# The last of an answer's twelve copies of transposed probabilities: from ScalarE to VectorE

## The reference

```
x = x + attention_0(x)    # layer norm, 16 heads of 64, one shared key/value head, a bias of 16x256x256,
                          # a mask of keys, a null key and value, a causal mask, softmax, output projection, norm
x = x + attention_1(x)    # the same form; q and k are normalized, the bias comes from a small MLP over distances
x = x + experts_2(x)      # 8 experts of 64 and a shared one of 128, two experts to a token
x = x + experts_3(x)
```

## Time and profile before

| | us |
|---|---|
| median of 3 runs | 357.94 |
| lowest, highest run | 357.38, 360.69 |
| the profiled execution, its own time | 356.2 |
| its span, first to last instruction | 354.4 |
| PE busy | 326.2 (92%) |
| DVE busy | 253.0 (71%) |
| ACT busy | 246.3 (69%) |
| POOL busy | 195.5 (55%) |

### The profile page before, as it was taken

One profiled execution on the slowest core, in us unless ns is written; L12 is line 12 of the kernel. 1 busy time (PEld: TensorE's weight loads), 2 busy tenths in 40 slices (PEclk: granted clock), 3 DMA queues, 4 the chain that ended last, 5 costly groups with the idle time before them and its releaser, 6 DMA issues.

```text
span 354.4 us, 7089 instructions
## 1 busy us (share of the span) xinstructions
PE 326.2 (92%) x2276; PEld 245.7 (69%) x2276; DVE 253.0 (71%) x917; ACT 246.3 (69%) x822; POOL 195.5 (55%) x282
## 2 busy tenths in 40 slices
PE   8789989997989999989997899989999899999996
PEld 6676756677667767766676567666767578676885
DVE  4668998896756677948785888578769536477672
ACT  2679876996788778969895879697886922232330
POOL 4591186479358866977498769786943502200000
PEclk9999999999999999999999999999999999999999
DMA  5961202320839500219110202021120200000001
GB/s 173 384 175 40 62 0 63 46 62 1 135 46 146 87 10 8 55 45 362 41 25 3 61 1 61 25 38 33 30 61 3 61 2 0 0 3 0 0 2 59
DMA packets 26653, 21.33 MB, mean 60 GB/s; under 512 B 2436, under 2 KB 25976, under 8 KB 26232
## 3 DMA queue, kind: packets, MB, share of 16 engines
q1 hardware_dynamic: 25624, 20.37, 23.0%
q10 hardware_dynamic: 992, 0.51, 1.1%
HBM read 19.84 MB, written 1.04 MB: 59 GB/s over the span
## 4 chain that ended last, share of the span: by engine, by line
PE 43%; POOL 19%; DVE 15%; ACT 12%; issue 7%; DMA 3%; ACTq 0%; SPq 0%; POOLq 0%; DVEq 0%
PE bank L1421 5%; PE bank L1442 5%; ACT sb_prob L785 4%; DVE sb_prob L1163 4%; POOL sb_nb L927 4%; POOL sb_oT L932 4%; POOL sb_rq L908 3%; PE bank L1360 3%; POOL sb_xn L876 3%; PE bank L1536 3%; PE bank L1532 2%; DMA sb_r_rows<-recip_rows 2%; PE bank L1413 2%; PE bank L1498 2%; PE bank L1300 2%
## 5 line engine op out<-in xcount | busy, mean ns | idle before, releaser
L785 ACT ACTIVATE sb_prob<-sb_prob,sb_low 128x128 f32<-128x128 f32 (+1 forms) x256 | 113.3, 449 | 4.7 <-DVE sb_low L1163 3.5
L793 ACT ACTIVATE sb_pT<-bank 128x512 f32<-128x512 f32 x96 | 54.3, 590 | 11.2 <-PE bank L1413 10.5
L1413 PE MATMUL bank<-sb_ident,sb_prob 128*128 128x128 f32 x384 | 56.5, 280 | 4.2 <-ACT sb_pT L793 1.5
L1413 PEld LDWEIGHTS bank<-sb_ident,sb_prob 128*128 128x128 f32 x384 | 41.9, 141 | 22.7 <-issue 8.5
L1421 PE MATMUL bank<-sb_pT,sb_v_a 128*64 128x512 f32 x192 | 48.3, 609 | 2.0 <-ACT sb_ln L806 1.9
L785 ACT ACTIVATION_READ_ACCUMULATOR sb_prob<-sb_prob,sb_low 128x1 f32 x256 | 49.7, 194 | 0.0
L932 POOL TENSOR_TENSOR sb_oT<-sb_oT,sb_r_rows 128x1024 f32<-128x1024 f32 x15 | 35.8, 2385 | 15.9 <-DMA sb_r_rows<-recip_rows 15.9
L1163 DVE CUSTOM_DVE_ANT_0 sb_prob<-bank,sb_nb,sb_t 128x128 f32<-128x128 f32 x128 | 38.6, 341 | 7.6 <-PE bank L1388 6.7
L908 POOL TENSOR_TENSOR sb_rq<-sb_ss,sb_minus_half 128x8 f32<-128x8 f32 x16 | 26.4, 1651 | 16.8 <-DVE sb_ss L1130 16.7
L1442 PE MATMUL bank<-sb_wo,sb_oT 128*128 128x128 f32 x256 | 32.0, 278 | 3.1 <-POOL sb_oT L932 2.9
L1442 PEld LDWEIGHTS bank<-sb_wo,sb_oT 128*128 128x128 f32 x256 | 30.0, 192 | 5.6 <-issue 4.5
(11 more groups left out here) (205 smaller groups left out, 769.3 us busy)
## 6 DMA issues: line engine op xcount, KB each, us to landing
sb_r_rows<-recip_rows SPq DMA_DIRECT2D x30, 256.0 KB, 4.2
sb_packed<-in_packed SPq DMA_DIRECT2D x1, 2992.0 KB, 12.4
sb_bias<-in_bias SPq DMA_DIRECT2D x1, 2048.0 KB, 13.8
sb_toep<-bias_table SPq DMA_DIRECT2D x8, 256.0 KB, 8.6
sb_stage<-in_L_cond_Wq SPq DMA_DIRECT2D x2, 512.0 KB, 5.5
sb_bias<-in_bias SPq DMA_DIRECT2D x1, 1024.0 KB, 8.9
sb_wo<-in_L_cond_Wo SPq DMA_DIRECT2D x1, 512.0 KB, 12.3
sb_wo<-in_L_cond_Wout SPq DMA_DIRECT2D x1, 512.0 KB, 6.2
```

The costliest lines, as they stand in the source:

```text
L785: act.activation(p[:, j], p[:, j], ACT.Exp, scale=-1.0, bias=low[:, buf, half, h:h + 1], accum_out=total[:, buf, half, h:h + 1]).then_inc( ...
L793: act.activation(pT[:, c % PT_SLOTS].rearrange("p j q -> p (j q)"), t_ring.bank("T", s, n)[:], ACT.Copy).then_inc(t_ring.frees("T", s, n), 1)
L1413: ins = pe.transpose(dst[:, j * P:j * P + P], p[:, j % 2, kb * P:kb * P + P], ident[:])
```

## The change

The tile n = 11 of every answer is copied by VectorE and no longer by ScalarE; the other eleven stay. That is 8 of 96 copies. The copy takes the same place in the list (`LATE` is the 0.05 that all copies have), so `ORDER` stays as it is, and it waits for the same two things: its tile transposed, its slot of `sb_pT` read. Since the copies of an answer now come from two engines, `V` waits for each of its tiles and not only for the last.

```diff
+BY_VECTOR = (11,)
+LATE = 0.05
...
-                put(here + to_t + 0.05, "T_hi", s, n)
+                put(here + to_t + (LATE if n in BY_VECTOR else 0.05), "T_hi", s, n)
...
-            if kind == "T_hi":                       # ScalarE
+            if kind == "T_hi" and n not in BY_VECTOR:
...
+            if kind == "T_hi" and n in BY_VECTOR:    # VectorE
+                c = len(TRANSPOSED) * s + n
+                w.wait_ge(*t_ring.filled("T", s, n))
+                if c >= PT_SLOTS:
+                    of, u = divmod(c - PT_SLOTS, len(TRANSPOSED))
+                    w.wait_ge(*o_ring.filled("V", of, four_of(u)))
+                dve.tensor_copy(pT[:, c % PT_SLOTS].rearrange("p j q -> p (j q)"), t_ring.bank("T", s, n)[:])\
+                    .then_inc(t_ring.frees("T", s, n), 1)
...
             if kind == "V":                          # TensorE
                 half = n // 2
-                w.wait_ge(*t_ring.emptied("T", s, tile_of(2 * n + 1, half)))
+                for kb in range(half + 1):
+                    for g in (2 * n, 2 * n + 1):
+                        w.wait_ge(*t_ring.emptied("T", s, tile_of(g, kb)))
```

## The result

The kernel after took 362.46 us (361.51 to 364.04, 4 runs) against 357.76 us (357.38 to 360.69, 4 runs): 1.0132 of the time before, 95% interval 1.008 to 1.0184. It lies above the forecast of 359.7 and above its range, which ended at 361.7. A repeat with more runs gave less than half of that: 361.05 against 359.43, ratio 1.0056 (1.0014 to 1.0098). Most of the rest goes with TensorE's clock, and about 1 us stays open.

A forecast was written before the change was run, and what follows sets the result against it. The prediction took hand-overs between engines to bound the kernel, with no engine deciding everything. Terms of 0 for s = 0 to 5, +1.14 at s = 6 and +0.60 at s = 7 gave +1.7, so 359.7 us; range 356.9 to 361.7.

The forecast's parts named there:

- The early six: Copies of answers s = 0 to 5: gains on ScalarE and delays on VectorE absorbed by waits or cancelling, sum 0.
- s = 0: First answer: ScalarE waits for TensorE anyway, VectorE's 0.60 us delay vanishes in 1.13 us of idle time; sum 0.
- s = 1, 4 and 5: Three answers where existing waits of ScalarE or VectorE cover the moved copy; sum 0 each.
- s = 3: Fourth answer: W_aggr 0.60 us late, L903 perhaps 0.4 late with slack behind it; sum 0 (0 to +0.4).
- s = 2, sum 0: Third answer: kv 0.40 us earlier, but W_aggr 0.47 later uses up GpSimd's 0.43 idle; between -0.40 and +0.04.
- s = 7, +0.60: Last answer: the copy delays the reciprocal, L942 and the last Z, without slack: +0.60 us (0 to +0.7).
- D: Rival: copies hold GpSimd, 0.60 us at s = 2, 3 and 4 on top: +3.6, 361.5 us; chance 0.04.
- s = 6, +1.14: VectorE waits at the copy ahead of the reciprocal; Z 1.49 us late, 0.35 absorbed before T(7.1): +1.14 (0.0 to +1.5).
- I take the difference from the median: Final step: the +1.7 us from the profiled execution (356.2) is added to the runs' median, 357.94, giving 359.7.
- A: Rival: ScalarE's relief pays 0.49 us each at s = 2 and s = 6, VectorE's stops absorbed: 357.0 us; chance 0.14.
- B: Rival: VectorE's lateness passes on in every answer, 0.60 at seven places, 1.49 at s = 6: +5.7, 363.6; chance 0.08.
- C: Rival: only s = 6 or only s = 7 is paid: +0.6 to +1.2, 358.5 to 359.1 us; chance 0.14.

The follow-up runs named there:

- the filled pair: Kernels after and before, both with added matmuls on zeros in TensorE's waits, four ahead of xt 6.0 included: 357.37 against 355.41 us, ratio 1.0055.
- the kernel before filled: Kernel before plus matmuls on zeros in TensorE's waits, four ahead of xt 6.0 included: 355.41 us, 0.9936 of the kernel before.
- the kernel after filled: Kernel after the change plus the same matmuls on zeros in TensorE's waits: 357.37 us, 0.9998 of the kernel before.
- the first filling: Kernel before plus matmuls on zeros ahead of kvn 0.0, q 0.3, Z 1.1, xt 3.0 and W 2.0, none in xt 6.0: 356.54 us, ratio 0.9965.
- the filled kernels: Kernels with matmuls on zeros added in TensorE's waits; with the fullest filling, before took 355.41 us and after 357.37.

## Why the prediction was wrong

**The steps.** The early six, sum 0: right within what the level can tell (+0.2 ± 0.5). s = 0 is a small miss, 0.16 us, by a slower instruction that no term had. s = 1, 4 and 5 move nothing in the filled pair; at s = 3 L903 is 0.4 late, as written, and that is taken up. s = 2, sum 0: right to about 0.1 us, and by the mechanism given; the kernel after:

```profile
124.11 0.67 DVE L1175 COPY sb_pT<-bank 128x512 f32<-128x512 f32 x1
...
124.70 0.17 DVE L1200 BATCH_NORM_AGGREGATE sb_out_mv<-sb_out_st 128x2 f32<-128x6 f32 x1
...
126.66 0.71 POOL L906 TENSOR_TENSOR sb_rk<-sb_ss_k,sb_minus_half 128x2 f32<-128x2 f32 x1
```

The aggregate waits behind the copy, and GpSimd's 0.43 us ahead of `rk` are gone; ScalarE's copy of `kv` came 0.40 earlier, and that was lost again behind it: in the filled pair and in the repeat L903 is 0.12 us later against TensorE's work, where the bound said 0.04. s = 7, +0.60: right to the hundredth. D: GpSimd's scaling of an answer has a mean of 2385 ns before and 2387 after, and the copies, 683 ns at the mean, match `O`. The Trainium skill, "VectorE: DVE Perf Modes", Why PSUM operands drop a tier, says that a PSUM operand rules out the mode that takes both of VectorE's SBUF read ports. By that, the trace agrees: 2385 and 2387 ns.

**s = 6, +1.14: the mechanism was right, the size wrong, +1.50.** The cause "that wait is taken up, so of the 1.49 us 1.14 stay" failed. The wait of 0.35 us ahead of T(7.1) was indeed taken up; but another limit ended at the same time. TensorE and ScalarE, the kernel before filled, then the kernel after filled:

```profile
261.00 1.42 PE L1413 MATMUL bank<-sb_ident,sb_prob 128*128 128x128 f32 x8
261.69 0.60 ACT L793 ACTIVATE sb_pT<-bank 128x512 f32<-128x512 f32 x1 [0.71 <-PE bank L1413]
262.34 1.06 PE L1481 MATMUL bank<-sb_packed,sb_xT 128*128 128x8 f32 x8
```

```profile
262.99 1.09 PE L1424 MATMUL bank<-sb_ident,sb_prob 128*128 128x128 f32 x8
263.68 0.60 ACT L796 ACTIVATE sb_pT<-bank 128x512 f32<-128x512 f32 x1 [1.37 <-PE bank L1424]
264.33 1.06 PE L1494 MATMUL bank<-sb_packed,sb_xT 128*128 128x8 f32 x8 [0.25 <-ACT sb_pT L796]
```

The eight transposes shrink from 1.42 to 1.09 us, which is the wait taken up. The logits' matmuls, next in the queue, need the bank of T(7.0). ScalarE begins to copy that bank 0.69 us after T(7.0) starts and takes 0.60 us, in both kernels. In either kernel the logits' matmuls start 1.34 us after the transposes do. T(7.0) had moved by the full 1.5, and so did they. A gap is slack only if nothing else ends where it ends.

**The step that put the time outside the range** is the last one: "I take the difference from the median". The profiled execution, 356.2 us, had a granted clock of 1.00 throughout, and the prediction carried the median's 1.7 us above it over to the kernel after as if they were fixed. They go with the clock: the medians of the kernel before move between 357.8 and 359.4 from set to set. The measured 362.46 us is 2.8 above the forecast. Of these, 0.4 are the term of s = 6. By the line of 3.27 us per 0.01, the four runs of the kernel after, with clocks of 0.985 to 0.991, carry some 3.6 us of lower clock, while the median that was built on, 357.94, lies 2.0 above the level of the kernel before; the difference, an estimate, is 1.6. The range counted costs of the change, and named the spread of runs only in passing, so it had no room for that. About 1 us is left, the first timing's level of +3.1 ± 0.8 against +2.0 ± 0.5. (The three add up to 0.2 or 0.3 too much; the line has a scatter of 0.8.) Whether that is chance, the slow transfer, or the early copies by way of it, stays open.

**The rivals.** A: no; at s = 6 the relief is worth nothing, at s = 2 it needs another place. B: not as stated; its +5.7 lies near the +4.7 of the first timing by accident, and in the filled pair its six early places cost at most 0.5 together, where it had 3.6. C: no, both are paid. D: no.

## What to carry to other kernels

An operation moved between engines costs what stands behind it in the new queue: the same two copies cost 2.1 us ahead of two reciprocals and nothing that a trace shows behind them. Look at each place on its own, and before you count a wait as slack, check when the next instruction's other inputs and its bank would let it start. Where runs differ by more than the effect, read the granted clock of each run first; filling TensorE's waits with work on zeros gave a measurement sharp enough to see 2 us, and was worth more (-0.6%, 0.9907 to 0.9965) than anything in the change.

## What of the hardware was not expected

- TensorE's clock fell from its upper to its lower level behind waits of only 0.8 to 2.9 us (0.81 us ahead of 14.96 us in the repeat of the kernel after, with a granted clock of 0.50 from 16 to 18 us; 2.91 us ahead of 119.86 us in its first trace), and not in each execution: the wait of 2.39 us at s = 4 stood in the kernel before with a clock of 1.00 as well as in the kernel with the first filling, where the next 6 us had 0.72. What decides between the two is open.
- The mean clocks of runs gathered near a few values (0.981, 0.986, 0.990, 0.995, 1.000), as if a run held a number of like falls. Each step of 0.005 went with some 1.6 us.
- The transfer of the softmax sums' rows (256 KB each, L671) at s = 2 was issued alike in each execution, two loads with four loads of another table right behind. The slower of the two landed 5.1 us after its issue in the kernel before, where GpSimd did not wait for it, and 8.7 us in the kernel after, where GpSimd waited 2.39 us. At this place the wait was at most 0.98 us in the filled kernels; that the filling is the reason was not tested, and neither was the part of the early copies.
